# A sum formed one stage earlier, one load less in a second product on two queues, and pieces of an output product put between other products

## The chip, the cores and the metric

One core of a Trainium2 chip runs the kernel. The figure is the device time of one launch in microseconds; of the kernel before there are three runs, and their median is 7700.91 (7690.25 to 7706.97). TensorE multiplies, VectorE (DVE), ScalarE (ACT) and GpSimd (POOL) compute elementwise, and transfers between HBM and on-chip memory are issued into queues by SyncE (SP), ScalarE and GpSimd and carried by 16 DMA engines.

## The reference

`x` has shape (2, 96, 256, 256). Layer 0 adds to `x` a transformer block on its group-normalised copy; layer 1 adds a clustering block. Cut to what matters:

```python
x = x + _L0_conv_ref(_gn(x), ...)    # layer 0
x = x + _L1_conv_ref(_gn(x), ...)    # layer 1, clustering

def _L0_conv_ref(x, ...):            # here x is _gn(x)
    # windows of 16x16, step 14, in 19 bands of 19 windows for each batch
    y = _layernorm(tok, norm1_w, norm1_b)
    attn = softmax(q @ k.T / 4)
    tok = (attn @ v) @ wproj + tok
    x2 = overlap_add(tok) * factors
    y = _gelu(_layernorm(x2) @ fc1_w + fc1_b)
    dw = _gelu(depthwise_5x5(y) + dw_b)
    y = y + dw
    return y @ fc2_w + fc2_b + x2

def _cluster_fwd(x, ...):            # f, v: 1x1 convolutions; 8 regions
    sim = sigmoid(beta + alpha * cos(centres, points))
    sim = sim * (one-hot of its maximum over the 4 centres)
    agg = (sim @ value + value_centres) / (sum(sim) + 1)
    return proj(agg.T @ sim)
```

So the input of layer 1, called x1 in the kernel, is the original input plus `x2` plus the second product of the MLP.

## The kernel before

The stages run one behind another, each in a block of its own with a barrier at its end: group-norm statistics, a small setup, layer norm (`layer_norm`, writes `y_attention`), `attention` (writes `x2`), `fc1` (writes `y_mlp`), `conv` (the depthwise convolution, writes `s_mlp`), `fc2` (the second product, writes `x1`), a setup of the clustering, and `cluster` (writes `out`). Within a block every engine runs a program written out by hand; semaphores order them. The order of the work is the order of the code: there is no scheduler.

`attention` goes through 38 bands (19 per batch) of 19 windows. `acc` holds, in two slots, the 16 rows of a band, 4096 numbers in each of 96 partitions. SP loads the rows of x into it (`load_x`), GpSimd scales them to the group-normalised input in pieces of two rows (`scale`, L534), adds each window's projected result (`add`, L557), and hands the last rows to the next band (L561). In each window GpSimd also multiplies the attention result by its reciprocals (`normalise`, L540 and L544), for which it waits for VectorE; in eight windows of a band it turns an eighth of the next band's columns (`turn_columns`, L527). SP stores the finished 14 rows as x2 when the band's last `add` is done, and also spreads queries and keys of the next band over the heads (`spread_heads`).

`fc2` works on 14 tiles of 5 or 4 blocks (`tile_rows`); a tile is two half tiles `v` (`jj` 0 or 1). A block gives, for each batch and each of two row pairs, two rows of 256 pixels. The partitions hold four groups `g` of 32 output channels; `g // 2` is the batch, and `grp` counts the three parts of the 96 channels. SP alone issues the loads: `load_x(k)` 12 transfers of x2 into `xa` and 12 of x into `xb`, each into 32 partitions, and `load_s(v)` the activations s in transfers into 128 partitions (`sa`) and 64 (`sbb`), with the pixels of a row kept in four phases `q` (pixel 4k+q). GpSimd adds `xb` to `xa` (L1297). TensorE multiplies chunks of two rows (512 columns), four products with `sa` and four with `sbb` for each `grp` (L1317, L1320); the moving operand is read in the order

```python
.rearrange("c q (t k b) -> c b t k q", t=count, b=B)[:, b, :, 0:COLS, :]
```

so that neighbouring columns lie a whole line of a phase apart (650 numbers, 2600 bytes), and the pixels come out in natural order. VectorE adds bias, product and `xa` (L1336) and sums for the next group norm (L1342); ScalarE squares (L1354) and then issues the 12 stores of a tile (L1361).

`cluster` goes through 4 halves `f` of 4 segments of 8 steps `u`. In a step TensorE forms the products of a unit (L1720, two halves of four products), which ScalarE reads out (L1805 to L1808) and VectorE norms (L1846). A segment later, at the steps of `TURN_AT` (two turns at steps 3, 4 and 5, one at 6 and 7), `turn` transposes and aggregates (L1737, L1743), VectorE copying the result into `smt` (L1875). One half later, `piece` multiplies `smt` with the weights of the half (L1768) and VectorE adds the result into `xv` (L1904): two pieces in each of 48 steps (`pieces_at`: steps 3 to 7 of three segments and step 3 of one, for three halves), and the 32 pieces of the last half one behind another at the end (`rest`). Each piece uses the same two banks, so it waits until VectorE has added the piece before. The last lines of a step are

```python
                for a in pieces:
                    piece(*a)
```

in TensorE's program and the same with `added` in VectorE's.

## Time and profile before

| | |
|---|---|
| median of three runs | 7700.91 us (7690.25 to 7706.97) |
| the profiled execution's own time | 7690.68 us |
| its span, from first to last instruction | 7688.9 us |
| busy: TensorE, VectorE, ScalarE, GpSimd | 6602.4, 4890.2, 3553.5, 2457.7 us |
| mean granted clock of TensorE, as a share of 2.4 GHz | 0.932 |
| moved by DMA | 1252.80 MB |

The profile is of one execution. A busy time is the time in which an instruction of the engine runs; idle time before an instruction is put down to what ended it (`<-`). PE is TensorE's products, PEld its weight loads. One product of 32-bit numbers is two PE instructions. L1317 is line 1317 of the kernel. Names of buffers are shortened: `f_` is `fc2` (and `fc1`), `cl_` and `c_` the clustering, `at_` attention; x there stands for x2 and x1 as well.

### The profile page before, as it was taken

Reading aid. Unit: us, or ns where it says so; the run is one execution under the profiler, and the core shown is the slowest. Engines: PE = TensorE matmul, PEld = TensorE weight load, DVE = VectorE, ACT = ScalarE, POOL = GpSimd, SP = SyncE. Lnnn points to the kernel's source line nnn. Section 1 sums busy time; section 2 is a strip of 40 time slices with the busy share of each in tenths; the row PEclk is TensorE's granted clock in tenths of the full one; section 3 lists DMA queues with packets and bytes.
Section 4 is the critical chain, followed back from the end, with each engine's and each line's share of the span. In section 5 each row is a group of like instructions: output and inputs, shape, how many; then the busy total and the mean of one; then the engine's idle time right before and its main releaser. Section 6 shows DMA issues by size and latency. Waiting matters only on the chain. (4 is left out here: it accounts for less than half of the span.)

```text
span 7688.9 us, 138214 instructions
## 1 busy us (share of the span) xinstructions
PE 6602.4 (86%) x52604; PEld 3232.1 (42%) x52604; DVE 4890.2 (64%) x7370; ACT 3553.5 (46%) x5600; POOL 2457.7 (32%) x3173
## 2 busy tenths in 40 slices
PE   0886999999999999999997898899957768688885
PEld 0332555555555555555553333555500000476662
DVE  6785777777777777777774555788812222454554
ACT  0553666666666666666664666344401101243330
POOL 0443444444444444444445565000012222000000
PEclk9997999999999999999998999999988989787885
DMA  7784333334333434333325886988799999345655
GB/s 300 196 239 124 77 77 78 88 85 91 79 71 73 88 83 92 83 77 77 78 46 155 254 250 206 359 342 344 282 249 274 248 272 250 97 112 140 172 147 164
DMA packets 480460, 1252.80 MB, mean 163 GB/s; under 512 B 159620, under 2 KB 164740, under 8 KB 442628
## 3 DMA queue, kind: packets, MB, share of 16 engines
q1 hardware_dynamic: 444276, 1141.72, 54.3%
q0 software_dynamic: 7168, 50.34, 2.1%
q10 hardware_dynamic: 28368, 51.91, 1.8%
q8 instruction: 431, 7.06, 0.4%
q14 instruction: 217, 1.78, 0.1%
HBM read 731.14 MB, written 458.07 MB: 155 GB/s over the span
## 5 line engine op out<-in xcount | busy, mean ns | idle before, releaser
L727 DVE TENSOR_REDUCE at_mz<-at_ps 128x4 bf16<-128x1024 f32 x1444 | 1774.6, 1229 | 782.5 <-PE at_ps L651 782.2
L600 ACT ACTIVATE at_E<-at_ps 128x1024 f32<-128x1024 f32 x1444 | 1500.9, 1040 | 794.7 <-PE at_ps L663 794.7
L663 PE MATMUL at_ps<-at_qaug,at_k 32*128 32x256 f32 x11552 | 830.0, 401 | 79.2 <-DVE at_qaug L751 79.2
L674 PE MATMUL at_ps<-at_E,at_vaug 128*32 128x256 f32 x11552 | 774.3, 386 | 0.0
L1190 PE MATMUL cv_ps<-cv_yin,cv_band 128*128 128x384 f32 x2304 | 745.4, 486 | 27.9 <-DMA cv_yin<-y_mlp 27.9
L1210 DVE TENSOR_TENSOR cv_yin<-cv_gl,cv_yin 64x384 f32<-64x384 f32 x1152 | 637.5, 553 | 150.8 <-ACT cv_gl L1201 142.9
L663 PEld LDWEIGHTS at_ps<-at_qaug,at_k 32*128 32x128 f32 x11552 | 523.1, 184 | 443.1 <-issue 224.5
L1297 POOL TENSOR_TENSOR f_xa<-f_xa,f_xb 128x3840 f32<-128x3840 f32 (+1 forms) x28 | 213.2, 7636 | 1544.1 <-DMA f_xb<-in_x 1544.1
L540 POOL TENSOR_TENSOR at_share<-at_rden,t_share 128x8 f32<-128x8 f32 x722 | 146.8, 203 | 1558.8 <-DVE at_rden L738 1558.6
L1336 DVE SCALAR_TENSOR_TENSOR f_xa<-f_ps,f_b,f_xa 128x512 f32<-128x512 f32 (+1 forms) x216 | 136.2, 687 | 753.6 <-PE f_ps L1320 753.6
L1317 PE MATMUL f_ps<-f_sa,f_wa 128*32 128x512 f32 (+1 forms) x1728 | 379.8, 958 | 268.2 <-DMA f_sbb<-s_mlp 268.2
L651 PE MATMUL at_ps<-at_k,at_q 32*128 32x256 bf16 x5776 | 579.1, 277 | 8.9 <-DMA at_k<-at_packed 7.4
L1190 PEld LDWEIGHTS cv_ps<-cv_yin,cv_band 128*128 128x128 f32 x2304 | 436.1, 189 | 337.5 <-DMA cv_yin<-y_mlp 28.8
L1201 ACT ACTIVATE cv_gl<-cv_ps,cv_bias 128x384 f32<-128x384 f32 x576 | 334.4, 581 | 438.2 <-PE cv_ps L1190 438.2
L1720 PE MATMUL cl_ps<-c_rhs,cl_xu 97*128 97x208 f32 x2048 | 504.1, 416 | 21.9 <-ACT cl_dots L1808 19.6
L1354 ACT ACTIVATE f_squared<-f_xa 128x1280 f32<-128x1280 f32 (+1 forms) x84 | 99.1, 1180 | 895.1 <-DVE f_xa L1336 893.3
L681 PEld LDWEIGHTS at_ps<-t_wv,at_y 96*128 96x128 f32 x2888 | 377.1, 190 | 297.8 <-issue 297.8
L1720 PEld LDWEIGHTS cl_ps<-c_rhs,cl_xu 97*128 97x128 f32 x2048 | 463.6, 239 | 86.6 <-issue 76.2
L557 POOL TENSOR_TENSOR at_acc<-at_prs,at_acc 96x256 f32<-96x256 f32 x722 | 495.3, 686 | 3.1 <-ACT at_prs L606 3.1
L681 PE MATMUL at_ps<-t_wv,at_y 96*128 96x96 f32 x2888 | 495.5, 294 | 0.1
L686 PE MATMUL at_ps<-at_ot,t_wproj_heads 128*96 128x256 f32 x1444 | 485.4, 418 | 2.2 <-ACT at_prs L606 1.8
L544 POOL TENSOR_TENSOR at_on<-at_turned,at_share 128x256 f32<-128x256 f32 x722 | 444.3, 615 | 105.5 <-DVE at_ot L744 2.6
(210 smaller groups left out, 9570.2 us busy)
## 6 DMA issues: line engine op xcount, KB each, us to landing
cv_yin<-y_mlp SPq DMA_DIRECT2D x48, 2340.0 KB, 14.7
s_mlp<-cv_yin SPq DMA_DIRECT2D x48, 2340.0 KB, 8.4
at_rows_in<-y_attention SPq DMA_DIRECT2D x38, 1536.0 KB, 9.4
gn_xin<-in_x SPq DMA_DIRECT2D x16, 3072.0 KB, 23.2
ln_xin<-in_x SPq DMA_DIRECT2D x192, 256.0 KB, 7.6
y_attention<-ln_xin SPq DMA_DIRECT2D x192, 256.0 KB, 3.8
cl_xu<-x SPq DMA_DIRECT2D x128, 384.0 KB, 3.8
cl_xv<-x SPq DMA_DIRECT2D x64, 768.0 KB, 5.5
```

The source lines that it names most:

```text
L544: pool.tensor_tensor(on[:, s, :].rearrange("p (a d) -> p a d", d=VC), turned[:, s, :].rearrange("p (a d) -> p a d", d=VC), share[:, s, :]. ...
L557: pool.tensor_tensor(a, prs[:, m % 2, :].rearrange("p (r c) -> p r c", c=PS), a, ALU.add).then_inc(added, 1)
L600: act.activation(E[:, m % 2, 2 * p:2 * p + 2, :], psum[:, 2 + 2 * p:4 + 2 * p, :], ACT.Exp).then_inc(exp_done, 1)
L651: i = pe.matmul(psum[:, g, TOK * j:TOK * j + TOK], q_upper[rows, n % 2, tokens(w, 128 * j, 128)], k_upper[rows, n % 2, tokens(w)], start=T ...
L663: i = pe.matmul(psum[:, 2 + h, TOK * j:TOK * j + TOK], k[rows, n % 2, tokens(w, 128 * j, 128)], qaug[rows, m % 2, :], start=True, stop=True)
L674: i = pe.matmul(pv_ps[32 * h:32 * h + VC, 0:TOK], vaug[:, m % 2, z, h, :], E[:, m % 2, h, z * TOK:(z + 1) * TOK], start=(z == 0), stop=(z ...
L681: i = pe.matmul(lin_ps[:, j * C:(j + 1) * C], y[0:C, n % 2, tokens(w, 128 * j, 128)], t["wv"][:], start=True, stop=True)
L686: pe.matmul(lin_ps[0:C, 0:TOK], t["wproj_heads"][:], ot[:, m % 2, :], start=True, stop=True).then_inc(proj_done, 1)
L727: dve.tensor_reduce(mz[:, m % 2].rearrange("p j (h c) -> p h j c", c=32)[:, 2 * p:2 * p + 2, :, DQ], psum[:, 0:2, :].rearrange("p h (j n) ...
L1190: m = pe.matmul(psum[:, n % NB, 0:3 * RUN], band[:, s, c, a, :], yin[:, s, c, 3 * u:3 * u + 3, GAP * a:GAP * a + RUN], start=(a == 0), sto ...
L1210: i = dve.tensor_tensor(yc, gl[half_rows(f), n % NG, :].rearrange("p (t n) -> p t n", n=RUN), yc, ALU.add)
L1720: m = pe.matmul(psum[:, 2 * half + g // 2, 256 * (g % 2):256 * (g % 2) + NFC], xu[:, n % XS, 128 * tile:128 * tile + 128], t["rhs"][:, f * ...
```

## The change

It has five parts.

1. `attention` also forms xs = x + x2. SP loads the finished rows of x a second time, into a new buffer `xr`; GpSimd adds `acc` to it in pieces of two rows (`both`), one per window from window 5 of the next band on, and all eight pieces of the last band behind its last window; SP stores `xr` as xs. The scaling of a band's fresh rows, until now one piece per window in the band before from window 11 on, is done in the first four windows of the band itself, two pieces in each.
2. `fc2` loads xs only: `xb` and GpSimd's addition are gone, and `xa` has three slots for two.
3. In `fc2` SP and ScalarE each issue half of the loads and half of the stores (batch 0, partitions 0 to 63, from SP; batch 1 from ScalarE; of s the one row pair each).
4. TensorE in `fc2` reads phase by phase ("phases outside"), in steps of two numbers, so that a row comes out in phase order; VectorE's addition then takes one row per instruction and puts each pixel in its place, in steps of four numbers.
5. In `cluster` the first piece of a step goes between the two halves of the products and the second between the two turns, in VectorE's program alike.

In the layer norm and in the clustering several semaphores are also merged into others that already counted the step before or after (`log_done` into `rs_done`; seven of the weights' chain into `lhs_steps` and `lhs_taken`); the waits stay in the same places.

```diff
@@ -488,17 +497,22 @@
             for i in range(YP // 2):
                 spread_heads(0, i)
             for n in range(NB + 1):
+                if n >= 1:
+                    rows = own_rows(n - 1)
+                    if n >= 2:
+                        sp.wait_ge(xs_stored, 16 * (n - 1))
+                    sp.dma_start(xr[:, 0:rows * W], rows_of(x, n - 1, 0, rows)).then_inc(xr_loaded, 16)
                 if n + 1 < NB:
                     spread_heads(n + 1, 0)
                 if n >= 1:
-                    r = (n - 1) % NWIN
                     sp.wait_ge(added, NWIN * n)
-                    rows = STEP if r < NWIN - 2 else 2 if r == NWIN - 2 else PS
                     sp.dma_start(rows_of(x2, n - 1, 0, rows), acc[:, (n - 1) % 2, 0:rows * W]).then_inc(stored, 16)
                 if n + 1 < NB:
                     spread_heads(n + 1, 1)
                     spread_heads(n + 1, 2)
                 if n >= 1:
+                    sp.wait_ge(summed, sums(n - 1))
+                    sp.dma_start(rows_of(xs, n - 1, 0, rows), xr[:, 0:rows * W]).then_inc(xs_stored, 16)
                     sp.wait_ge(stored, 16 * n)
                     if n + 1 < NB:
                         if carries(n):
...
@@ -560,6 +575,13 @@
                     pool.wait_ge(added, m + 1)
                     pool.tensor_copy(acc[:, (n + 1) % 2, 0:(PS - first) * W], acc[:, n % 2, first * W:]).then_inc(carried, 1)
+            def both(n, piece):
+                if piece == 0:
+                    pool.wait_ge(added, NWIN * (n + 1))
+                    pool.wait_ge(xr_loaded, 16 * (n + 1))
+                rows = slice(piece * 2 * W, (piece + 1) * 2 * W)
+                pool.tensor_tensor(xr[:, rows], xr[:, rows], acc[:, n % 2, rows], ALU.add).then_inc(summed, 1)
             for piece in range(YP):
                 turn_columns(0, piece)
             for piece in fresh(0):
@@ -570,11 +592,15 @@
                 if n >= 5:
                     add(n - 5)
                 nb, w = where(n)
-                if nb + 1 < NB:
-                    if 2 <= w < 2 + YP:
-                        turn_columns(nb + 1, w - 2)
-                    if w >= 11 and w - 11 < len(fresh(nb + 1)):
-                        scale(nb + 1, fresh(nb + 1)[w - 11])
+                if nb + 1 < NB and 2 <= w < 2 + YP:
+                    turn_columns(nb + 1, w - 2)
+                if 1 <= nb < NB:
+                    for piece in fresh(nb)[2 * w:2 * w + 2]:
+                        scale(nb, piece)
+                    if 5 <= w < 5 + own_rows(nb - 1) // 2:
+                        both(nb - 1, w - 5)
+            for piece in range(own_rows(NB - 1) // 2):
+                both(NB - 1, piece)
         @block.scalar
...
@@ -1228,19 +1255,51 @@
+        def load_x(queue, k, half):
+            count = tile_rows(k)[2]
+            if k >= XA:
+                queue.wait_ge(stored[k % XA], 16 * XLOADS * (k // XA))
+            for grp in range(CGRP):
+                for rr in range(2):
+                    g = 2 * half + rr
+                    queue.dma_start(xa[32 * g:32 * g + 32, k % XA, grp, 0:count].rearrange("c t j w -> c t (j w)"),
+                                    group_rows(xs, k, half, rr, grp)).then_inc(xa_loaded[k % XA], 16)
+        def load_s(queue, v, half):
+            for row, t, at, count in row_sources(v // 2, half, v % 2):
+                n = count * PITCH - GAP
+                run = slice(at * PITCH, at * PITCH + n)
+                for f in range(2):
+                    src = sdr[:, f, row, :, t:t + count, :].rearrange("c e t n -> c e (t n)")[:, :, GAP * f:GAP * f + n]
+                    queue.dma_start(sa[:, v % 2, half, 2 * f:2 * f + 2, run], src[0:128]).then_inc(s_loaded[v % 2], 16)
+                    queue.dma_start(sbb[64 * half:64 * half + 64, v % 2, 2 * f:2 * f + 2, run], src[128:MLP]).then_inc(s_loaded[v % 2], 16)
+        def store(queue, k, half):
+            count = tile_rows(k)[2]
+            queue.wait_ge(x1_done, first[2 * k + 2])
+            queue.wait_ge(squares_done, CGRP * (2 * k + 2))
+            queue.wait_ge(sums_done, 2 * k + 2)
+            for grp in range(CGRP):
+                for rr in range(2):
+                    g = 2 * half + rr
+                    queue.dma_start(group_rows(x1, k, half, rr, grp),
+                                    xa[32 * g:32 * g + 32, k % XA, grp, 0:count].rearrange("c t j w -> c t (j w)")).then_inc(stored[k % XA], 16)
         @block.sync
         def _(sp):
...
@@ -1250,51 +1309,19 @@
...
+            load_x(sp, 0, 0)
+            load_s(sp, 0, 0)
+            load_s(sp, 1, 0)
             for k in range(NTILE):
                 if k + 1 < NTILE:
+                    load_x(sp, k + 1, 0)
+                    sp.wait_ge(f_done, first[2 * k + 1])
+                    load_s(sp, 2 * k + 2, 0)
+                    sp.wait_ge(f_done, first[2 * k + 2])
+                    load_s(sp, 2 * k + 3, 0)
+                store(sp, k, 0)
+            for u in range(XA):
+                sp.wait_ge(stored[u], 16 * XLOADS * len(range(u, NTILE, XA)))
...
@@ -1304,7 +1331,7 @@
                 def lines(a, b):
-                    return a[:, :, b0 * PITCH:b0 * PITCH + count * PITCH].rearrange("c q (t k b) -> c b t k q", t=count, b=B)[:, b, :, 0:COLS, :]
+                    return a[:, :, b0 * PITCH:b0 * PITCH + count * PITCH].rearrange("c q (t k b) -> c b t q k", t=count, b=B)[:, b, :, :, 0:COLS]
...
@@ -1327,41 +1354,50 @@
-                if n == first[v]:
-                    dve.wait_ge(xs_done, v + 1)
+                if n == first[v] and jj == 0:
+                    dve.wait_ge(xa_loaded[k % XA], 16 * XLOADS * (k // XA + 1))
                 dve.wait_ge(f_done, n + 1)
                 for grp in range(CGRP):
-                    xc = xa[:, k % 2, grp, b0:b0 + count, jj, :]
-                    pc = psum[:, CGRP * (n % 2) + grp, 0:count * W].rearrange("p (t w) -> p t w", w=W)
-                    i = dve.scalar_tensor_tensor(out=xc, in0=pc, scalar=b2[:, grp:grp + 1], in1=xc, op0=ALU.add, op1=ALU.add)
+                    for row in range(count):
+                        xc = xa[:, k % XA, grp, b0 + row, jj, :].rearrange("p (k q) -> p q k", q=PHASES)
+                        pc = psum[:, CGRP * (n % 2) + grp, row * W:row * W + W].rearrange("p (q k) -> p q k", q=PHASES)
+                        i = dve.scalar_tensor_tensor(out=xc, in0=pc, scalar=b2[:, grp:grp + 1], in1=xc, op0=ALU.add, op1=ALU.add)
                 i.then_inc(x1_done, 1)
                 if n + 1 == first[v + 1]:
                     dve.wait_ge(x1_done, n + 1)
...
+            load_x(act, 0, 1)
+            load_s(act, 0, 1)
+            load_s(act, 1, 1)
+            for k in range(NTILE):
+                if k + 1 < NTILE:
+                    load_x(act, k + 1, 1)
+                    act.wait_ge(f_done, first[2 * k + 1])
+                    load_s(act, 2 * k + 2, 1)
+                squares(2 * k)
+                if k + 1 < NTILE:
+                    act.wait_ge(f_done, first[2 * k + 2])
+                    load_s(act, 2 * k + 3, 1)
+                squares(2 * k + 1)
+                store(act, k, 1)
+            for u in range(XA):
+                act.wait_ge(stored[u], 16 * XLOADS * len(range(u, NTILE, XA)))
...
@@ -1772,8 +1806,16 @@
             for seg, u, turns, pieces in steps():
                 f, s = seg // SU, seg % SU
                 if seg < SEGS:
-                    products(seg * UPS + u)
-                for a in turns:
+                    products(seg * UPS + u, 0)
+                for a in pieces[0:1]:
+                    piece(*a)
+                if seg < SEGS:
+                    products(seg * UPS + u, 1)
+                for a in turns[0:1]:
+                    turn(*a)
+                for a in pieces[1:2]:
+                    piece(*a)
+                for a in turns[1:2]:
                     turn(*a)
                 if f and s == 0 and u == UPS - 1:
                     combined(f - 1)
...
@@ -1910,10 +1948,18 @@
                 if seg and u == 0:
                     similar(seg - 1)
                 if seg < SEGS:
-                    norms(seg * UPS + u)
+                    norms(seg * UPS + u, 0)
+                for a in pieces[0:1]:
+                    added(*a)
+                if seg < SEGS:
+                    norms(seg * UPS + u, 1)
                 if seg and u == 0:
                     choose(seg - 1)
-                for a in turns:
+                for a in turns[0:1]:
+                    turned(*a)
+                for a in pieces[1:2]:
+                    added(*a)
+                for a in turns[1:2]:
                     turned(*a)
                 if f and s == 0 and u == UPS - 1:
                     normalised(f - 1)
```

Three places show how the rows of an engine's program stand before and after; a row names the line, the operation, the buffers and the shape, and `x6` counts equal rows.

SP's program in `fc2` before, from the last transfers of one half tile's s to the next: `f_xa` and `f_xb` are the buffers of x2 (shown as `x`) and x (`in_x`), `f_sa` and `f_sbb` those of s.

```order
L1277 DMA f_sa<-s_mlp 128x2x648
L1278 DMA f_sbb<-s_mlp 64x2x648
L1259 DMA f_xa<-x 32x4x512 x12
L1265 DMA f_xb<-in_x 32x4x512 x12
L1277 DMA f_sa<-s_mlp 128x2x518
L1278 DMA f_sbb<-s_mlp 64x2x518
```

And ScalarE's after, at the same tile (SP's has the same transfers for batch 0, without the squares of L1382): L1301 stores a tile, L1279 loads xs.

```order
L1301 DMA x<-f_xa 32x4x512 x6
L1279 DMA f_xa<-xs 32x4x512 x6
L1289 DMA f_sa<-s_mlp 128x2x518
L1290 DMA f_sbb<-s_mlp 64x2x518
L1289 DMA f_sa<-s_mlp 128x2x518
L1290 DMA f_sbb<-s_mlp 64x2x518
L1382 ACTIVATE f_squared,squares<-f_xa 128x1280 x3
L1289 DMA f_sa<-s_mlp 128x2x518
L1290 DMA f_sbb<-s_mlp 64x2x518
L1289 DMA f_sa<-s_mlp 128x2x518
L1290 DMA f_sbb<-s_mlp 64x2x518
L1382 ACTIVATE f_squared,squares<-f_xa 128x1280 x3
```

The loads of s are shared out over two programs, the 12 transfers of `xb` are gone, and the stores now stand in both programs ahead of the loads of the tile after the next one.

TensorE's program in a step of `cluster` with two turns, before: L1720 is `products`, L1737 and L1743 a turn, L1768 two pieces.

```order
L1720 MATMUL cl_ps<-c_rhs,cl_xu 128x208 x8
L1737 MATMUL cl_ps<-c_eye,cl_sm 16x128 x8
L1743 MATMUL cl_ps<-cl_val,cl_sm 16x97 x8
L1737 MATMUL cl_ps<-c_eye,cl_sm 16x128 x8
L1743 MATMUL cl_ps<-cl_val,cl_sm 16x97 x8
L1768 MATMUL cl_ps<-cl_smt,cl_lhs 96x512 x4
```

And after, where the same lines are L1754, L1771, L1777 and L1802:

```order
L1754 MATMUL cl_ps<-c_rhs,cl_xu 128x208 x4
L1802 MATMUL cl_ps<-cl_smt,cl_lhs 96x512 x2
L1754 MATMUL cl_ps<-c_rhs,cl_xu 128x208 x4
L1771 MATMUL cl_ps<-c_eye,cl_sm 16x128 x8
L1777 MATMUL cl_ps<-cl_val,cl_sm 16x97 x8
L1802 MATMUL cl_ps<-cl_smt,cl_lhs 96x512 x2
L1771 MATMUL cl_ps<-c_eye,cl_sm 16x128 x8
L1777 MATMUL cl_ps<-cl_val,cl_sm 16x97 x8
```

The two pieces no longer stand next to each other, and the two turns have a piece between them.

GpSimd's program in `attention`, windows 11 and 12 of a band before (L540 and L544 `normalise`, L557 `add`, L534 `scale`):

```order
L540 TENSOR_TENSOR at_share<-at_rden,t_share 128x8
L544 TENSOR_TENSOR at_on<-at_turned,at_share 128x256
L557 TENSOR_TENSOR at_acc<-at_prs,at_acc 96x16x16
L534 TENSOR_SCALAR at_acc<-at_acc,t_gn_scale,t_out_shift 96x512
L540 TENSOR_TENSOR at_share<-at_rden,t_share 128x8
```

And after, windows 2 and, after the dots, 5 of the band itself (L555 and L559 `normalise`, L572 `add`, L542 `turn_columns`, L549 `scale`, L583 `both`):

```order
L555 TENSOR_TENSOR at_share<-at_rden,t_share 128x8
L559 TENSOR_TENSOR at_on<-at_turned,at_share 128x256
L572 TENSOR_TENSOR at_acc<-at_prs,at_acc 96x16x16
L542 COPY at_y<-at_rows_in 96x512
L549 TENSOR_SCALAR at_acc<-at_acc,t_gn_scale,t_out_shift 96x512 x2
...
L555 TENSOR_TENSOR at_share<-at_rden,t_share 128x8
L559 TENSOR_TENSOR at_on<-at_turned,at_share 128x256
L572 TENSOR_TENSOR at_acc<-at_prs,at_acc 96x16x16
L542 COPY at_y<-at_rows_in 96x512
L583 TENSOR_TENSOR at_xr<-at_xr,at_acc 96x512
```

Two scalings and a column turn now share a window, and a sum takes the place of the scaling beside the later column turns.

## Rows read from the trace of the kernel before

**Rows 1.** The view of windows by stage: us, busy time (and count) by engine, clock, DMA share, GB/s.

```profile
637.00:4080.00 3443.00, 3319.80 (x35264) 1709.62 (x35264) 2588.91 (x4335) 2126.93 (x3192) 1592.25 (x2765) 0.99 0.36 79
5590.00:6588.00 998.00, 728.73 (x3456) 68.13 (x3456) 246.19 (x300) 106.85 (x168) 213.23 (x28) 0.87 0.98 253
6571.00:6588.00 17.00, 0.00 (x0) 0.00 (x0) 3.36 (x3) 3.33 (x6) 0.00 (x0) 0.50 0.62 185
6640.00:7555.00 915.00, 746.71 (x6513) 593.03 (x6512) 474.69 (x768) 313.95 (x831) 23.95 (x47) 0.82 0.51 138
7555.00:7689.00 134.00, 70.16 (x174) 14.97 (x174) 49.70 (x77) 0.00 (x0) 8.59 (x17) 0.52 0.60 182
```

**Rows 2.** The same view, of stretches with one kind of transfer.

```profile
20.00:120.00 100.00, 0.00 (x0) 0.00 (x0) 94.56 (x158) 0.00 (x0) 0.00 (x0) 1.00 1.00 430
4900.00:5500.00 600.00, 600.00 (x1860) 351.31 (x1859) 514.57 (x930) 269.83 (x465) 0.00 (x0) 1.00 0.89 344
5600.00:5630.00 30.00, 0.00 (x0) 0.00 (x0) 0.00 (x0) 0.00 (x0) 6.58 (x1) 0.50 1.08 231
6180.00:6190.00 10.00, 0.00 (x0) 0.00 (x0) 0.00 (x0) 0.00 (x0) 10.00 (x2) 0.50 1.05 400
```

**Rows 3.** DMA of the second product, by queue: packets, MB, share of 16 engines.

```profile
q1 hardware_dynamic: 104259, 201.77, 83.7%
q10 hardware_dynamic: 27264, 50.34, 13.7%
```

**Rows 4.** Groups by line, second product (L1018: `fc1`): busy us, mean ns | idle, releaser.

```profile
L1317 PE MATMUL f_ps<-f_sa,f_wa 128*32 128x512 f32 x1344 | 328.5, 1057 | 268.2 <-DMA f_sbb<-s_mlp 268.2
...
L1018 PE MATMUL f_ps<-f_x,f_w 32*128 32x512 f32 x1344 | 168.3, 632 | 20.9 <-ACT f_ya L1057 20.8
...
L1336 DVE SCALAR_TENSOR_TENSOR f_xa<-f_ps,f_b,f_xa 128x256 f32<-128x256 f32 x48 | 20.3, 479 | 62.5 <-PE f_ps L1320 62.5
```

**Rows 5.** Groups by line, VectorE: a contiguous row, an addition of a piece, steps of 16 bytes.

```profile
L751 DVE TENSOR_TENSOR at_qaug<-at_ps,at_q 128x256 f32<-128x256 f32 x722 | 306.6, 425 | 57.8 <-PE at_ps L693 3.9
...
L1904 DVE SCALAR_TENSOR_TENSOR cl_xv<-cl_ps,c_proj_b,cl_xv 96x512 f32<-96x512 f32 x256 | 179.8, 742 | 183.4 <-PE cl_ps L1768 183.4
...
L1863 DVE TENSOR_TENSOR cl_hit<-cl_hit 128x256 f32<-128x256 f32 x16 | 10.0, 625 | 0.5
```

**Rows 6.** Groups by line, GpSimd, in attention and (L298) in the layer norm.

```profile
L527 POOL COPY at_y<-at_rows_in 96x512 f32<-96x512 f32 x304 | 325.9, 1073 | 4.9 <-DMA at_rows_in<-y_attention 4.9
...
L544 POOL TENSOR_TENSOR at_on<-at_turned,at_share 128x256 f32<-128x256 f32 x722 | 444.3, 615 | 105.5 <-DVE at_ot L744 2.6 <-POOL at_share L540 0.4
...
L534 POOL TENSOR_SCALAR at_acc<-at_acc,t_gn_scale,t_out_shift 96x512 f32<-96x512 f32 x256 | 195.8, 765 | 172.3 <-DMA at_acc<-in_x 172.3
...
L298 POOL TENSOR_TENSOR ln_sq<-ln_xin 128x1536 f32<-128x1536 f32 x64 | 175.7, 2746 | 289.1 <-DVE ln_xin L354 289.1
```

**Rows 7.** Timeline of GpSimd in attention: start us, us, instruction [idle before <- releaser].

```profile
1753.10 0.20 POOL L540 TENSOR_TENSOR at_share<-at_rden,t_share 128x8 f32<-128x8 f32 x1 [2.01 <-DVE at_rden L738]
...
1754.02 0.73 POOL L557 TENSOR_TENSOR at_acc<-at_prs,at_acc 96x256 f32<-96x256 f32 x1
...
1757.43 0.20 POOL L540 TENSOR_TENSOR at_share<-at_rden,t_share 128x8 f32<-128x8 f32 x1 [1.93 <-DVE at_rden L738]
```

**Rows 8.** DMA issues: count, KB each, median us to landing.

```profile
at_acc<-in_x SPq DMA_DIRECT2D x34, 1344.0 KB, 8.9
```

**Rows 9.** Timeline of TensorE in the clustering, four steps of two or one turns.

```profile
7068.99 3.08 PE L1720 MATMUL cl_ps<-c_rhs,cl_xu 97*128 97x208 f32 x16
...
7241.96 4.76 PE L1720 MATMUL cl_ps<-c_rhs,cl_xu 97*128 97x208 f32 x16
...
7248.31 0.63 PE L1737 MATMUL cl_ps<-c_eye,cl_sm 128*16 128x128 f32 x16 [0.70 <-DVE cl_smt L1875]
...
7251.82 1.10 PE L1768 MATMUL cl_ps<-cl_smt,cl_lhs 16*96 16x512 f32 x4 [1.51 <-DVE cl_xv L1904]
...
7285.42 0.80 PE L1720 MATMUL cl_ps<-c_rhs,cl_xu 97*128 97x208 f32 x3
```

162 lines of the change are left out of this document (57 added, 105 removed).

## The prediction, made before the changed kernel ran

> **What bounds the kernel now.** I read the stages first, from the view of windows [rows 1]. Attention takes 3443 us with TensorE busy for 3320 of them at a granted clock of 0.99, and its DMA engines are busy only 0.36 of the time. The second product (`fc2`, from the end of the convolution to 6588 us) takes 998 us with the DMA engines at a share of 0.98 and only 253 GB/s; TensorE is busy for 729 of them. The clustering loop takes 915 us, TensorE busy 747 and the clock 0.82; after it stand 134 us of pieces alone. The change touches these three stages. The rest (statistics, layer norm, `fc1`, convolution) keeps its instructions. There, and in the clustering, semaphores are merged into one another with the same order of increments, which I cost at nothing: the producers already follow one another.
>
> Next, why 0.98 of the DMA time moves only 253 GB/s. In [rows 2] the same 16 engines moved 430 GB/s at the start, where each load fills 128 partitions, and 344 over 600 us of the convolution, loads and stores of 128 partitions mixed. In the first 30 us of `fc2`, where nothing but loads of x2 and x into 32 partitions at a time is in flight, they are full (1.08) and give 231. And at 6180, where ACT's queue stores x1 (32 partitions too) while SP's queue loads, the same full engines give 400. So full engines do not mean a full rate, and a second queue beside SP's has gone with a high one. The queue view [rows 3] says the same over the stage: SP's queue carries 201.8 MB in 0.837 of 1000 us (241 GB/s), ACT's 50.3 MB in 0.137 (367 GB/s).
>
> **fc2, DMA.** Of the 252.1 MB it drops the load of x, 50.3 (as much as the x1 stores that ACT's queue carries), and leaves 201.8 MB [rows 3]. With nothing else changed the loads would need 837 us less 50.3 MB at 231 GB/s (218 us), so 619, and the stores 137: 756 us. At 400 GB/s throughout it would be 505 us. The two queues now each load half the batch into other partitions (0 to 63 from SP, 64 to 127 from ACT), which no stretch here shows with loads alone on both. I take 335 GB/s, just under the convolution's 344, since most loads of s fill 128 partitions as there, and the x loads, which do not, are a quarter of the bytes. That gives 602 us. About 20 us stand around it, where little can be in flight: the last half tile through TensorE, VectorE, ScalarE and its store, now 17 us at a DMA share of 0.62 behind the last product (6571 to 6588 in [rows 1]). Together 622 us, 376 less than 998.
>
> **fc2, does an engine become the bound?** The 14 tiles hold 64 blocks (eight tiles of five, six of four), so a tile of five is 15.8 MB, 47 us at 335 GB/s.
> TensorE: four products of 512 columns are eight instructions, 1344 instructions cost 328.5 us, so 1.96 us for eight [rows 4]. A tile of five blocks has 24 such groups and 12 of 256 columns, 30 in all by halves, 59 us: over 47. But the new order of the moving operand runs through k first, in steps of 8 bytes, where the old one jumped 2600 bytes at every element. `fc1`'s product of the same 512 columns, read without gaps, costs 168.3 us for 1344 instructions [rows 4]. By that row the stage's TensorE work falls from 729 to 373 us and a tile to 30. A step of 8 bytes stands between the two rows; I take the nearer, the contiguous one, and keep 729 as the other end.
> The Trainium skill (SBUF — State Buffer, Door 1) says that two accesses within one 16-byte line keep the full rate; by it the 8-byte step costs nothing and the stage is at 373, and without it at 729. No row here has that step.
> VectorE: 216 additions become 384 of one row each, read and written in steps of 16 bytes. A contiguous one of 256 elements takes 479 ns now [rows 4]; the nearest row with steps of 16 bytes has 625 ns where a contiguous one has 425 [rows 5], so I take 680 ns. All 384 are then 261 us (184 at 479 ns); even with the whole of today's 246 us [rows 1] left beside them VectorE has 507 us of work in 622. ScalarE is busy for 107 of 998 us [rows 1] and takes over half of the loads' issues, 20 per tile; an issue that lasts waits for room behind transfers, and hides under them. The third buffer of x lets a store come one tile late. So none of them is the bound, and since a tile's products need 30 of its 47 us, the buffers of s are free again well before the queues run dry.
>
> **Attention.** GpSimd adds 256 sums `both` of 96x512, and the 256 scalings move to the first four windows of a band. From 615 ns for 256 elements and 2746 for 1536 [rows 6] one `both` is about 1.05 us. GpSimd waits about 2 us in a window of 4.33 for the reciprocals [rows 7]. The fullest window after (column turn and two scalings) holds 0.20+0.62+0.65+1.07+2x0.77 = 4.1 us; the sums fall into windows without scalings, 3.6 us of work. `normalise` is needed one window later, so 0.1 us of lateness costs nothing. DMA: 100.7 MB more in 3443 us, from 79 to 108 GB/s on engines at 0.36, hidden. SP waits for the sums of a band before the next x load, but that is at window 11, and the load (8.9 us [rows 8]) is wanted seven windows of 4.33 us later. If that cover were gone, each band would pay the load, 37 x 9 us. What shows is the end: eight sums of the last band before the last store, +8.4 us, say 9.
>
> **Clustering.** 48 steps carry two pieces each. [rows 9] begins with one, at 7241.96: products 4.76 us (the 16 instructions take 3.08 at full clock, at 7068.99), two turns of some 1.1 us (the first half of one 0.63) with a wait of 0.70 for `smt` between them, a piece of 1.10, a wait of 1.51 for VectorE's two additions (0.74 each [rows 5]), a piece. In the new order products or a turn stand between the pieces, and a piece between the two turns: 2.5 us of TensorE's work against 1.5 of VectorE's, so both waits are covered. Waits alone: 48 x 1.51 and 27 x 0.70, 91 us. Products of 4.76 run in part at 1.2 GHz, behind those waits; the stage has 0.82 [rows 1]. If the clock holds at 2.4 GHz once they are gone, a step of two turns takes 3.0+2.2+2.2 = 7.4 us and one of one turn 6.3: four steps 27.4 against the 43.5 from 7241.96 to 7285.42 [rows 9]. Nine segments are 145 us, the 12 other steps at 2.2 us of waits 26: 171. The rows do not tell which; I take the middle, 130. The last 134 us, pieces alone, keep their order and time.
>
> **Sum.** 7690.7 (profiled execution) + 9 - 376 - 130 = 7194. That execution is 10 us under the median shown, 7700.9, so I forecast 7204, rounded to 7205.
>
> **Rivals.**
> *A, the forecast* (0.58): 7090 to 7290.
> *B, the second queue does not help the loads* (0.25). For it: all engines are full already at 231 GB/s [rows 2], and the 400 was a load beside a store, not two loads. Against: half-filled partitions are all that the 231 and the 430 differ in. Then `fc2` is 756+20 = 776 us, and the total 7690.7+9-222-130+10, about 7358.
> The Trainium skill speaks for B: SBUF — State Buffer ("Can I just issue two DMAs to hit both halves?") measured only 6% more for two loads at partitions 0 and 64, and DMA: Bandwidth & Descriptors (Rules for kernel authors) says that spreading over queues saves issue time alone. By them B's 7358 holds.
> *C, the 8-byte step reads as slowly as the old one* (0.06). For it: no row with that step. Then TensorE is busy 729 us at 59 us per tile, over the DMA's 47; with 25 us ahead and 20 behind, 774: about 7356.
> *D, the clustering gains nothing* (0.08): pieces and products share VectorE's queue, and an addition that waits for its piece now holds back the norms of the second half. Then the total is 7690.7+9-376+10, about 7334.
> *E, slower than before* (0.02). `both` waits in GpSimd's queue at window 5 for the load of x; behind it stand `normalise` and `add`, and behind them TensorE. It covers one window, 4.3 us, and would have to lose the whole gain, 497 us, over 37 bands, so the load must land 17.7 us late in each. It is issued some ten windows ahead (over 40 us) and takes about 9 us, like the present one; against it, then, a reserve of over 30 us.
> The change not doing what it says has 0.01: the load of x is gone from the queue's order.
>
> **How the numbers follow.** The time is A's. Best corner: 505+20 in `fc2` (-473) and -171, with 9 and 10 added 7066; worst of B with the waits alone, about 7400. Range 7090 to 7400: it leaves out the best corner, and C or B together with D. A alone reaches from 7090 to 7290. A measurement of this kernel tells about 0.2% (15 us) from no change. Faster 0.97 (A to D), same 0.01, slower 0.02 (E).
>
> **What the profile after would show.** `fc2` with one load of x per tile, in about 620 us at a DMA share near 1 and above 320 GB/s; under 280 GB/s B is right. The product of 512 columns under 700 ns instead of 1057 [rows 4]; if over 1000, C. VectorE's one-row addition at 480 to 680 ns. In attention the window still 4.33 us, with no wait of GpSimd for `xr`, and 9 us more at the end. In the clustering no 1.51 us waits ahead of the pieces but in the tail, and steps of 7.4 and 6.3 us if the granted clock rises from 0.82 to near 1. The forecast is wrong if the loads on two queues stay below 280 GB/s, or if issues held by a full queue keep ScalarE from its squares so long that stores, and with them the x buffers, come late.

## The result and the profile after

The changed kernel takes 7233.65 us (median of four runs, 7221.24 to 7236.30); the kernel before, with one run more than stated above, 7695.58 (four runs, 7675.86 to 7706.97). The ratio is 0.9392 with a 95% interval of 0.9372 to 0.9411. The forecast was 7205, with 7090 to 7290 for its own case. The profiled execution took 7235.98 us, its span 7234.2: 454.7 less than the span before.

The view of windows by stage, of the changed kernel: us, busy time (and count) of TensorE, its weight loads, VectorE, ScalarE and GpSimd, granted clock, DMA share, GB/s. The rows are attention, the first 33 us of `fc2`, `fc2`, the clustering loop and its tail.

```profile
634.00:4108.00 3474.00, 3332.49 (x35264) 1714.43 (x35264) 2588.90 (x4335) 2127.70 (x3192) 1907.13 (x3021) 0.98 0.47 107
5607.00:5640.00 33.00, 0.00 (x0) 0.00 (x0) 0.00 (x0) 0.00 (x0) 0.00 (x0) 0.50 1.01 248
5616.00:6294.00 678.00, 438.02 (x3456) 69.27 (x3456) 336.52 (x468) 106.83 (x168) 0.00 (x0) 0.82 1.01 297
6346.00:7100.00 754.00, 656.69 (x6515) 517.97 (x6513) 472.66 (x768) 315.57 (x831) 23.96 (x47) 0.91 0.59 168
7100.00:7234.00 134.00, 70.31 (x182) 14.98 (x174) 50.01 (x77) 0.00 (x0) 8.59 (x17) 0.52 0.60 182
```

Beside [rows 1] the reader sees three changes. `fc2` goes from 998 us to 678 (5616 to 6294), its DMA engines as full as before (1.01 for 0.98) but at 297 GB/s for 253. The clustering loop goes from 915 us to 754, TensorE's clock from 0.82 to 0.91; the tail stays at 134. And attention is longer, 3474 for 3447 (from its first to its last instruction, 3474.7 for 3446.8).

From the first to the last instruction of each stage:

| stage | before | after | difference | forecast |
|---|---|---|---|---|
| attention | 3446.8 | 3474.7 | +28 | +9 |
| `fc2` | 1006.6 | 686.8 | -320 | -376 |
| `cluster` | 1054.5 | 893.4 | -161 | -130 |
| all others together | 2180.1 | 2178.5 | -2 | 0 |

The queues of the second product, of the changed kernel (packets, MB, share of 16 engines), to set beside [rows 3]: each carries half, and together they take the whole of the engines' time.

```profile
q1 hardware_dynamic: 52432, 101.28, 50.9%
q10 hardware_dynamic: 51441, 99.81, 49.5%
```

The groups by line of the changed kernel: busy us, mean ns of one | idle before it, and what ended that. L1344 is the product of 512 columns, L1364 VectorE's one-row addition, L583 GpSimd's sum `both`.

```profile
L1344 PE MATMUL f_ps<-f_sa,f_wa 128*32 128x512 f32 x1344 | 204.1, 680 | 239.9 <-DMA f_sbb<-s_mlp 238.3 <-DVE f_xa L1364 1.5
...
L1364 DVE SCALAR_TENSOR_TENSOR f_xa<-f_ps,f_b,f_xa 128x256 f32<-128x256 f32 x384 | 227.0, 667 | 345.7 <-PE f_ps L1347 344.9
...
L583 POOL TENSOR_TENSOR at_xr<-at_xr,at_acc 96x512 f32<-96x512 f32 x256 | 323.9, 1266 | 0.1
```

The product fell from 1057 ns to 680 and the addition takes 667 (680 was forecast). TensorE waits 238 us for `sbb`, so the transfers still set the length of the stage. The sum `both` costs 1.27 us where 1.05 was taken.

A step of the clustering with two turns, from TensorE's timeline of the changed kernel (start us, us, instruction):

```profile
6800.94 1.67 PE L1754 MATMUL cl_ps<-c_rhs,cl_xu 97*128 97x208 f32 x8
6802.54 1.10 PE L1802 MATMUL cl_ps<-cl_smt,cl_lhs 16*96 16x512 f32 x4
6803.57 1.67 PE L1754 MATMUL cl_ps<-c_rhs,cl_xu 97*128 97x208 f32 x8
6805.18 0.63 PE L1771 MATMUL cl_ps<-c_eye,cl_sm 128*16 128x128 f32 x16
6805.62 0.52 PE L1777 MATMUL cl_ps<-cl_val,cl_sm 128*16 128x97 f32 x16
6806.07 1.10 PE L1802 MATMUL cl_ps<-cl_smt,cl_lhs 16*96 16x512 f32 x4
6807.10 0.63 PE L1771 MATMUL cl_ps<-c_eye,cl_sm 128*16 128x128 f32 x16
6807.55 0.52 PE L1777 MATMUL cl_ps<-cl_val,cl_sm 128*16 128x97 f32 x16
6807.99 1.67 PE L1754 MATMUL cl_ps<-c_rhs,cl_xu 97*128 97x208 f32 x8
```

No row has an idle time before it. The step lasts 7.06 us (6800.94 to 6808.00), where in [rows 9] four steps took 43.5; the steps of one turn last 6.16. The waits of the same stage, from the chain of waits (us in total, times, longest):

```profile
PE cl_ps L1754 <- DMA cl_xu<-x: 33.6, 10, 5.2
...
PE cl_ps L1771 <- DVE cl_smt L1913: 16.1, 19, 2.2
...
PE cl_ps L1802 <- DVE cl_xv L1942: 1.8, 2, 1.1
```

The wait of a piece for its additions has gone to 1.8 us. Another has grown: ten times the products wait for their load, 33.6 us in all, where it was 2.2 before.

### The profile page after: what moved, and what is told of

The parts are those of the page before. It is cut to its first block and busy times, and to the rows that moved or that the text cites. A ratio compares the mean times of both kernels' runs of the same rounds, so it can differ in the third digit from the quotient of the medians.

```text
span 7234.2 us, 138671 instructions
## 1 busy us (share of the span) xinstructions
PE 6229.6 (86%) x52604; PEld 3161.5 (44%) x52604; DVE 4977.8 (69%) x7538; ACT 3555.8 (49%) x5600; POOL 2561.1 (35%) x3401
## 3 DMA queue, kind: packets, MB, share of 16 engines
q8 instruction: 432, 7.08, 0.4%
q14 instruction: 219, 1.79, 0.1%
## 5 line engine op out<-in xcount | busy, mean ns | idle before, releaser
L555 POOL TENSOR_TENSOR at_share<-at_rden,t_share 128x8 f32<-128x8 f32 x722 | 146.9, 204 | 1444.7 <-DVE at_rden L764 1444.6
L572 POOL TENSOR_TENSOR at_acc<-at_prs,at_acc 96x256 f32<-96x256 f32 x722 | 495.1, 686 | 3.1 <-ACT at_prs L632 3.1
L559 POOL TENSOR_TENSOR at_on<-at_turned,at_share 128x256 f32<-128x256 f32 x722 | 444.1, 615 | 104.4 <-DVE at_ot L770 1.3
L1754 PE MATMUL cl_ps<-c_rhs,cl_xu 97*128 97x208 f32 x2048 | 445.4, 375 | 40.1 <-DMA cl_xu<-x 33.6
L1364 DVE SCALAR_TENSOR_TENSOR f_xa<-f_ps,f_b,f_xa 128x256 f32<-128x256 f32 x384 | 227.0, 667 | 345.7 <-PE f_ps L1347 344.9
L1754 PEld LDWEIGHTS cl_ps<-c_rhs,cl_xu 97*128 97x128 f32 x2048 | 395.1, 210 | 109.8 <-issue 67.3
L1344 PE MATMUL f_ps<-f_sa,f_wa 128*32 128x512 f32 (+1 forms) x1728 | 236.3, 619 | 239.9 <-DMA f_sbb<-s_mlp 238.3
L632 ACT ACTIVATE at_prs<-at_ps 96x256 f32<-96x256 f32 x722 | 426.9, 591 | 3.9 <-PE at_ps L712 3.6
```

Source lines behind the costliest of these rows:

```text
L559: pool.tensor_tensor(on[:, s, :].rearrange("p (a d) -> p a d", d=VC), turned[:, s, :].rearrange("p (a d) -> p a d", d=VC), share[:, s, :]. ...
L572: pool.tensor_tensor(a, prs[:, m % 2, :].rearrange("p (r c) -> p r c", c=PS), a, ALU.add).then_inc(added, 1)
L1754: m = pe.matmul(psum[:, 2 * half + g // 2, 256 * (g % 2):256 * (g % 2) + NFC], xu[:, n % XS, 128 * tile:128 * tile + 128], t["rhs"][:, f * ...
```

## The experiments

Each experiment is one edit of the changed kernel (the transfers by themselves are a program of their own). Its total is set against the changed kernel's 7233.65 us, but the kernel before, measured beside the experiments again, had medians of 7703 to 7707 us in place of 7696: differences of some 10 us between totals say little. Spans of stages are from one profiled execution each; where a stage's program is unchanged they show how far chance goes. `fc2` took 682 to 691 us in the four kernels in which it is the changed kernel's (692 and 701 in two where it reads x2), attention 3473 to 3484 in nine, the clustering 887 to 893 in ten.

### One queue for the loads

All loads of `fc2` on SP, all stores on ScalarE, as before; xs, the third buffer and the phases outside stay.

```diff
...
-                    load_x(sp, k + 1, 0)
-                    sp.wait_ge(f_done, first[2 * k + 1])
-                    load_s(sp, 2 * k + 2, 0)
-                    sp.wait_ge(f_done, first[2 * k + 2])
-                    load_s(sp, 2 * k + 3, 0)
-                store(sp, k, 0)
+                    for half in range(2):
+                        load_x(sp, k + 1, half)
+                    for v in (2 * k + 2, 2 * k + 3):
+                        sp.wait_ge(f_done, first[v - 1])
+                        for half in range(2):
+                            load_s(sp, v, half)
...
```

> The changed kernel, but all loads of the second product issued by SP and all its stores by ScalarE, as before the change; xs, three buffers of x and the phases outside stay. Theory P (the engines are full whichever queue feeds them, and the stage is as long as its packets take): the stage grows from 687 us by no more than what 248 against 231 GB/s does to the 50 MB of x, 15 us; 7235 to 7250 in all. Theory Q (loads into both halves of the partitions at once are what makes them faster): the stage goes to the 776 us of rival B, about 7322 in all.

Measured: 7291.74 us (7283.27 to 7306.23), and 750.0 us for `fc2`. The window of the stage in this kernel:

```profile
5616.00:6366.00 750.00, 441.03 (x3456) 69.27 (x3456) 336.02 (x469) 106.84 (x168) 0.05 (x1) 0.79 1.02 271
```

The engines are full (1.02) and give 271 GB/s for 297. So the second queue is worth 63 us: the 15 of theory P are too few, the 89 of Q too many. P rested on the 248 GB/s of the first 33 us, in which SP still loads weights; from 5620 to 5640, with both queues loading, the changed kernel moves 288. The other 257 of the 320 us come from the dropped load and what goes with it (the reading order, the third buffer); they are not split further here.

### Phases inside again

TensorE reads k innermost, VectorE adds two rows at once.

```diff
-...rearrange("c q (t k b) -> c b t q k", t=count, b=B)[:, b, :, :, 0:COLS]
+...rearrange("c q (t k b) -> c b t k q", t=count, b=B)[:, b, :, 0:COLS, :]
```

> The changed kernel, but TensorE reads k innermost in jumps of 2600 bytes again and VectorE adds in chunks of two rows, as before the change. If TensorE's 438 us become the 729 of before, a tile of five blocks needs 59 us of TensorE against 49 of DMA, and the stage grows from 687 to 775 or more: 7320 or more in all. If the transfers alone set the stage (theory P with TensorE hidden), it stays within 10 us of 7234.

Measured: 7354.77 us (7348.06 to 7360.23), `fc2` 807.4. The window and the product's group in this kernel:

```profile
5617.00:6424.00 807.00, 728.29 (x3456) 67.90 (x3456) 246.15 (x300) 106.86 (x168) 0.00 (x0) 0.95 0.80 252
```

```profile
L1344 PE MATMUL f_ps<-f_sa,f_wa 128*32 128x512 f32 x1344 | 328.3, 1056 | 71.4 <-DMA f_sbb<-s_mlp 71.4
```

TensorE is busy for 728 of 807 us and the DMA share falls to 0.80: the bound has changed sides. Once the transfers had shrunk, the new reading order, with VectorE's additions that go with it, was worth 121 us. With the transfers of before it would have been hidden, as far as the busy time tells (729 of 998); no run shows that.

### The clustering's order back

Both pieces at the end of a step, in both programs; the rest as changed.

```diff
-                for a in pieces[0:1]:
-                    piece(*a)
                 if seg < SEGS:
                     products(seg * UPS + u, 1)
-                for a in turns[0:1]:
-                    turn(*a)
-                for a in pieces[1:2]:
-                    piece(*a)
-                for a in turns[1:2]:
+                for a in turns:
                     turn(*a)
...
+                for a in pieces:
+                    piece(*a)
```

> The changed kernel, but both pieces of a step stand at its end again, behind the turns, in TensorE's and VectorE's programs. If the order is the whole cause of the 161 us that the clustering lost, its span is 1054 us again and the time about 7395. If a part came from elsewhere (merged semaphores, what the second product leaves behind), less.

Measured: 7412.02 us (7401.65 to 7433.63), the clustering 1057.9. The chain of waits of the stage in this kernel:

```profile
PE cl_ps L1802 <- DVE cl_xv L1938: 70.9, 47, 1.5
PE cl_ps L1771 <- DVE cl_smt L1909: 34.3, 45, 2.2
```

The 70.9 us are back, and the stage has its old length (1054.5). The order is the whole cause, within the few us by which a stage varies; the merged semaphores cost and gain nothing that shows. The total is 17 us over the 7395 expected, of which the clustering has 3.

### The second piece last

```diff
-                for a in pieces[1:2]:
-                    piece(*a)
                 for a in turns[1:2]:
                     turn(*a)
...
+                for a in pieces[1:2]:
+                    piece(*a)
```

> The changed kernel, but the second piece of a clustering step stands at the step's end, behind both turns; the first stays between the products. The wait of the second turn for the copy of the first is open again (0.70 us in 27 steps), the wait of a piece for the additions is still covered. By waits alone 19 us more, 7253. If such a wait also brings TensorE's clock down, as behind the waits of before, the steps of two turns grow beyond 7.8 us and the time beyond 7275.

Measured: 7256.71 us (7251.52 to 7274.23), 23 more than the changed kernel. Steps of two turns take 7.82 us for 7.06. TensorE's timeline of such a step:

```profile
6805.15 0.63 PE L1771 MATMUL cl_ps<-c_eye,cl_sm 128*16 128x128 f32 x16
6805.60 0.52 PE L1777 MATMUL cl_ps<-cl_val,cl_sm 128*16 128x97 f32 x16
6806.81 0.63 PE L1771 MATMUL cl_ps<-c_eye,cl_sm 128*16 128x128 f32 x16 [0.70 <-DVE cl_smt L1913]
```

The wait of 0.70 is open again, and everything round it is as short as in the changed kernel: a half of the products 1.67 us, a piece 1.10. So one such wait costs about its own length in its step, and the clock stays. The steps that carry pieces are 19 us longer together, as the waits alone gave; the others are 8 us shorter in this execution, and the whole clustering is 904.4 for 893.4. In the kernel before, steps with both kinds of wait went in part at half clock; whether the waits of 1.51 us alone would do that, no run tells.

### Attention without its sum, and with the sum but not its transfers

In the first kernel attention is that of before, and `fc2` reads x2, so x is missing from x1. (Its diff, long, takes out all that part 1 of the change put in.)

> The changed kernel with the attention of before: no xs is formed, and the second product loads x2 in its place, so that x is missing from x1. The transfers of the second product are as large as in the changed kernel. If attention's 28 us more are the price of the sum, 7206; if 18 of them are chance of the one execution and only the last band's sums cost, 7225.

Measured: 7213.80 us (7206.90 to 7230.09), between the two expected values; the span of attention decides, 3445.6. The three executions without the sum's transfers have 3446 to 3447, the ten with them 3473 to 3487: so the 28 us are the price of forming xs, not chance; in the nine kernels with the same attention it is 27 to 37.

The second keeps GpSimd's program and SP's wait for it, and takes away the 100 MB:

```diff
-                    sp.dma_start(xr[:, 0:rows * W], rows_of(x, n - 1, 0, rows)).then_inc(xr_loaded, 16)
...
-                    sp.dma_start(rows_of(xs, n - 1, 0, rows), xr[:, 0:rows * W]).then_inc(xs_stored, 16)
...
-                pool.tensor_tensor(xr[:, rows], xr[:, rows], acc[:, n % 2, rows], ALU.add).then_inc(summed, 1)
+                pool.tensor_tensor(xr[:, rows], acc[:, n % 2, rows], acc[:, n % 2, rows], ALU.add).then_inc(summed, 1)
```

> The changed kernel, but attention's 256 sums add the finished rows to themselves: x isn't loaded a second time and xs isn't stored (the second product reads x2, and x is missing from x1). GpSimd's work, its order, and SP's wait for the sums ahead of the next band's load of x stay. If the 18 us of attention's 28 that lie ahead of its last band come from the 100 MB more that fill the DMA engines in windows 14 to 18, they go, and only the last band's sums stay: attention 3456, 7215 in all. If they come from GpSimd's fuller windows or from the later load of x, attention stays at 3475 and the time at 7234.

Measured: 7212.40 us (7196.51 to 7220.82), attention 3446.1. The windows of attention in this kernel:

```profile
637.00:4083.00 3446.00, 3317.79 (x35264) 1708.26 (x35264) 2587.72 (x4335) 2128.55 (x3192) 1852.34 (x3021) 0.99 0.37 79
```

GpSimd is busy for 1852 us in place of before's 1593 (1907 in the changed kernel, since a sum of one input twice takes 1.00 us for 1.27) and attention isn't a microsecond longer. The whole price hangs on the transfers. The 3456 expected for attention, 10 us more, were missed: here the last band's eight sums, 8.01 us, run beside the last store of x2 and are hidden. The price has two parts. At the end, in the changed kernel's timeline of GpSimd and SP, the eight last sums stand ahead of one more store:

```profile
4091.07 0.30 SPq L509 DMA_DIRECT2D x<-at_acc  x1
4091.12 9.79 POOL L583 TENSOR_TENSOR at_xr<-at_xr,at_acc 96x512 f32<-96x512 f32 x8
4100.93 0.30 SPq L515 DMA_DIRECT2D xs<-at_xr  x1
```

The last store starts 9.8 us later than x2's does; the forecast had 8.4, say 9. It is the store behind the sums that makes them show. The other 18 us lie in windows 14 to 18 of a few bands. The windows around one (band 21), and TensorE's timeline there, of the changed kernel:

```profile
2630.00:2635.00 5.00, 4.81 (x58) 2.67 (x56) 4.17 (x10) 3.20 (x6) 1.80 (x5) 1.00 0.99 202
2635.00:2640.00 5.00, 3.74 (x26) 1.51 (x22) 1.78 (x3) 1.41 (x3) 1.11 (x2) 0.78 1.06 171
2640.00:2645.00 5.00, 5.00 (x40) 2.80 (x42) 3.11 (x5) 1.47 (x3) 1.50 (x3) 0.50 0.99 226
```

```profile
2635.34 0.70 PE L689 MATMUL at_ps<-at_qaug,at_k 32*128 32x256 f32 x5 [0.18 <-DVE at_qaug L777]
...
2637.12 1.44 PE L689 MATMUL at_ps<-at_qaug,at_k 32*128 32x256 f32 x11 [1.07 <-issue]
```

In the midst of 16 equal products, with no data to wait for, TensorE stands still for 1.07 us; then its clock falls to 0.50 of 2.4 GHz, and that window takes 8.55 us in place of 4.33. The DMA engines are full (0.99 to 1.06): behind the wait for the sums SP issues the store of xs, the load of x, keys and queries, the load of y, the tap blocks and the second load of x one after the other, in one stretch of some 30 us. With the wait but without the 100 MB there is no such gap; the 100 MB without the wait were not tried.

What TensorE stands still for can be read from the packets of the queue that carries its instructions (q8 in the view of DMA). In band 21 one packet starts at 2613.0 and the next only at 2633.5, where the median distance is 11.5 us. It has landed at 2635.6, and TensorE goes on at 2637.12. The view of DMA from 2633 to 2636 has it (packets, MB, share of 16 engines); the view from 2614 to 2633 has none of q8:

```profile
q8 instruction: 1, 0.02, 4.4%
```

All five such gaps of 0.7 us or more in the changed kernel's attention end 1.3 to 1.8 us after an instruction packet has landed that came 17.5 to 20.5 us behind the one before it; over all kernels with the 100 MB it is 63 of 63 gaps, 1.3 to 2.0 us after a landing, where a moment of attention taken at random lies 1 to 2 us after one in some 9% of cases. So TensorE had run out of instructions, and the next ones came late.

### The tap blocks out of that stretch

```diff
                 if n >= 1:
+                    unroll_taps((n - 1) * PER_BAND, PER_BAND)
                     sp.wait_ge(added, NWIN * n)
...
-                if n >= 1:
-                    unroll_taps((n - 1) * PER_BAND, PER_BAND)
```

> The changed kernel, but SP issues the four transfers of the convolution's tap blocks of a band ahead of its wait for the band's last addition (about window 5), and no longer behind the loads of x and y (windows 14 to 18), where TensorE stood still for lack of instructions in six bands. If the long stretch of full DMA engines there is what holds its instructions back, these stalls go and attention falls from 3475 by 10 to 20 us: 7215 to 7225. If they come from the number of transfers in a band, they move to other windows and the time stays at 7234.

Measured: 7243.89 us (7240.97 to 7250.35), attention 3486.6. The expectation fell, and so did its rival, by which the stalls would have moved to other windows: more windows were late (16 by over 1 us, 6 in the changed kernel), again all among windows 14 to 18. Attention is 12 us longer than in the changed kernel, but only 3 above the longest of the same attention in the other kernels. Which transfer of the stretch matters isn't settled. What the traces add: in several of these kernels the gap stands at the same place of TensorE's program (band 5 window 15, 16 window 15, 21 window 14, 22 window 14, 31 window 15), in others partly elsewhere, and in no execution without the 100 MB is there one of 0.7 us or more.

### The transfers by themselves

Sixteen kinds of transfer behind one another, some 5 MB each, with a barrier between; nothing is computed. This program was executed once.

```diff
+        phase("a_one_queue_32", p32((0, 2, 1, 3), S), [])
+        phase("b_two_queues_halves", p32((0, 1), S), p32((2, 3), S))
+        phase("c_two_queues_mixed", p32((0, 2), S), p32((1, 3), S))
...
+        phase("g_one_queue_32_spread", [spread(s, j) for s in S for j in range(4)], [])
```

> The transfers of the second product by themselves, one kind behind another with a barrier between, from x and a filled tensor shaped as s; nothing is computed, and the output holds copies of parts of x. Some 5 MB of each: 32 partitions a transfer on one queue; on two queues, each its half of the partitions; on two queues, halves mixed; 128 and 64 partitions a transfer with the same pieces of 2048 bytes; 32 partitions spread over all 128; 32 partitions in pieces of 10 KB; s into 128 partitions on one and two queues; s into 64 on one and two; stores on one and two; a load beside a store. If the partitions that a transfer covers set its rate: 231 GB/s for 32 adjoining ones, 400 or more for 128, and for 32 spread ones also near 400. If what it reads in HBM sets it (pieces of 2048 bytes a channel apart): 231 in all of these, and only the pieces of 10 KB are fast. If a second queue with the other half is what helps: 231 on one queue, over 350 on two with halves, 231 on two mixed.

Windows from the middle of each phase, where the engines are full (us, no engine busy, clock, DMA share, GB/s). In order: 32 adjoining partitions on one queue; on two, each its half; on two, halves mixed; 128 partitions; 64 on one queue; 64 on two, each its half; 32 spread over all 128; 32 in pieces of 10 KB; s into 128 on one queue, on two; s into 64 on one, on two; s into 128 and 64 in turn on one queue, and the part of that in which the two alternate; stores on one queue, on two; loads into 32 on one queue beside stores from 32 on the other.

```profile
44.00:62.00 18.00, 0.00 (x0) 0.00 (x0) 1.00 1.07 235
69.00:81.00 12.00, 0.00 (x0) 0.00 (x0) 1.00 1.06 333
88.00:106.00 18.00, 0.00 (x0) 0.00 (x0) 1.00 1.07 226
114.00:124.00 10.00, 0.00 (x0) 0.00 (x0) 1.00 1.05 402
130.00:150.00 20.00, 0.00 (x0) 0.00 (x0) 1.00 1.07 217
157.00:169.00 12.00, 0.00 (x0) 0.00 (x0) 1.00 1.05 333
177.00:188.00 11.00, 0.00 (x0) 0.00 (x0) 1.00 1.00 367
195.00:213.00 18.00, 0.00 (x0) 0.00 (x0) 1.00 1.02 221
221.00:230.00 9.00, 0.00 (x0) 0.00 (x0) 1.00 1.04 400
237.00:246.00 9.00, 0.00 (x0) 0.00 (x0) 1.00 1.04 399
253.00:272.00 19.00, 0.00 (x0) 0.00 (x0) 1.00 1.06 228
279.00:292.00 13.00, 0.00 (x0) 0.00 (x0) 1.00 1.04 311
299.00:318.00 19.00, 0.00 (x0) 0.00 (x0) 1.00 1.02 226
299.00:313.00 14.00, 0.00 (x0) 0.00 (x0) 1.00 1.03 238
325.00:341.00 16.00, 0.00 (x0) 0.00 (x0) 1.00 0.94 259
348.00:359.00 11.00, 0.00 (x0) 0.00 (x0) 1.00 1.03 352
366.00:376.00 10.00, 0.00 (x0) 0.00 (x0) 1.00 1.05 375
```

The source in HBM is out: pieces of 10 KB are no faster (221) than those of 2048 bytes (235), and the same pieces go at 367 when the 32 partitions are spread and at 402 when 128 are filled. Nor is it the number of partitions: 64 adjoining ones are no faster than 32 (217, 235). What counts is how they are spread, and over how much of the 128 what is in flight reaches at a time. A second queue helped the loads into 32 or 64 partitions when each queue kept to its half (333, 333 and 311; 226 with halves mixed, tried for 32 alone) and did nothing for those into 128 (400, 399). The stores gain in the same way (259, 352), and loads of 32 beside stores of 32, each on a queue of its own, reach 375. And wide transfers in turn with those into 64 partitions lose their advantage: 238 for the mix, where 400 and 228 for the shares of each would give 320 (an estimate from these rows). The longer window, 226, also holds the last four transfers into 64 partitions, which run by themselves.

### Halves mixed in the kernel

```diff
-                for rr in range(2):
-                    g = 2 * half + rr
+                for b in range(2):
+                    g = 2 * b + half
...
-                                    group_rows(xs, k, half, rr, grp)).then_inc(xa_loaded[k % XA], 16)
+                                    group_rows(xs, k, b, half, grp)).then_inc(xa_loaded[k % XA], 16)
```

> The changed kernel, but of xs SP loads the first row pair of both batches (partitions 0 to 31 and 64 to 95) and ScalarE the second, so that neither queue keeps to a half of the partitions; the loads of s and the stores stay. If the 63 us that the second queue is worth come from each queue keeping to its half, the second product goes from 687 us towards the 750 of one queue: 7260 to 7300. If it is the mixing of transfers of different kinds, no change: within 15 us of 7234.

Measured: 7284.17 us (7277.68 to 7285.40), `fc2` 730.9: 44 of the 63 us of the second queue go when the loads of x no longer keep to halves. That agrees with 333 and 226 above.

### Wide loads first

```diff
-            for row, t, at, count in row_sources(v // 2, half, v % 2):
...
+            for wide in (True, False):
+                for row, t, at, count in row_sources(v // 2, half, v % 2):
...
+                        if wide:
+                            queue.dma_start(sa[:, v % 2, half, 2 * f:2 * f + 2, run], src[0:128]).then_inc(s_loaded[v % 2], 16)
+                        else:
+                            queue.dma_start(sbb[64 * half:64 * half + 64, v % 2, 2 * f:2 * f + 2, run], src[128:MLP]).then_inc(s_loaded[v % 2], 16)
```

> The changed kernel, but each queue issues the loads of a half tile's s into 128 partitions first and then those into 64, in place of one after the other in turn. By the transfers measured alone, 67 MB into 128 partitions at 376 GB/s are 179 us and 34 MB into 64 on two queues at 295 are 114: 293 us for s in place of the 379 that its packets take now. If what is in flight at once sets the rate, and the two queues keep roughly in step, the second product falls by 40 to 86 us: 7148 to 7194. If only the mean over all partitions counts, nothing changes: within 15 us of 7234.

Measured: 7216.70 us (7201.67 to 7221.64), `fc2` 668.9: 18 us less, and 13 less than the shortest of the unchanged `fc2`, but under half of the lower bound. The order within a queue does little, presumably since the other queue is elsewhere; that wasn't shown.

### s in every second partition

The 64 channels go to partitions 0, 2, 4, ... (SP) and 1, 3, 5, ... (ScalarE); the weights of the other row pair are zero.

```diff
-                    queue.dma_start(sbb[64 * half:64 * half + 64, v % 2, 2 * f:2 * f + 2, run], src[128:MLP]).then_inc(s_loaded[v % 2], 16)
+                    queue.dma_start(sbb[half:128:2, v % 2, 2 * f:2 * f + 2, run], src[128:MLP]).then_inc(s_loaded[v % 2], 16)
...
-                        m = pe.matmul(psum[32 * g:32 * g + 32, bank, 0:w], wb[rows, outs], lines(sbb[rows, v % 2], g // 2), start=False, stop=True)
+                        m = pe.matmul(psum[32 * g:32 * g + 32, bank, 0:w], wb[:, g % 2, outs], lines(sbb[:, v % 2], g // 2), start=False, stop=True)
```

> The changed kernel, but the 64 channels of s that fill half the partitions lie in every second partition (even from SP, odd from ScalarE) in place of a lower and an upper half; TensorE multiplies them over all 128 partitions by weights that are zero for the other row pair. If the partitions that a transfer covers set its rate, as for the 32 spread ones (333 GB/s for 229), all of s moves at some 375 GB/s, 269 us in place of 379, and the second product falls by 70 to 110 us, if TensorE's products are not longer: 7124 to 7164. If the number of partitions counts and not where they lie, no change: 7234.

Measured: 7140.35 us (7134.32 to 7151.13); the ratio to the kernel before is 0.9263 (0.9240 to 0.9286). `fc2` takes 590.7 us. Its window and the two products in this kernel:

```profile
5609.00:6199.00 590.00, 383.96 (x3456) 123.02 (x3456) 336.24 (x468) 106.87 (x168) 0.11 (x1) 0.83 1.01 344
```

```profile
L1350 PE MATMUL f_ps<-f_sa,f_wa 128*32 128x512 f32 x1344 | 202.8, 671 | 197.5 <-DMA f_sbb<-s_mlp 188.6 <-DVE f_xa L1369 8.9
...
L1352 PE MATMUL f_ps<-f_sbb,f_wb 128*32 128x512 f32 x1344 | 198.0, 655 | 0.0
```

The same bytes with the same full engines (1.01) go at 344 GB/s for 297, and the product over 128 partitions costs 655 ns, no more than the other. The time lies within the 7124 to 7164 expected, so it is where the partitions lie that counts, and this version beats both kernels.

### Two buffers of x

```diff
-    XA = 3
+    XA = 2
```

> The changed kernel with two buffers of x in the second product, as before the change. SP's and ScalarE's queues then wait, ahead of a tile's loads of x, for the landing of the stores that stand right before them (12 to 19 us from issue to landing), with nothing else behind them in flight. If that empties the queues, 12 tiles lose some 13 us each: about 7390. If the loads of s that are still in flight cover it, less than 20 us: 7234 to 7254.

Measured: 7256.19 us (7243.59 to 7270.07), `fc2` 714.1 at a DMA share of 0.95: just above the range of the second case, and 23 us more than the longest of the unchanged `fc2`. The third buffer is worth some 25 us. The loads of s in flight cover most of the wait for the stores.

## Why the prediction was right, point by point

**What bounds the kernel.** Right: full engines at a low rate. The changed kernel shows 297 GB/s at 1.01, and the transfers alone show that the partitions are the reason why the stretch of 32 gave 231 and that of 128 gave 430 [rows 2]. That "half-filled partitions are all that the 231 and the 430 differ in" was not so when it was written: the pieces differed in length as well, and only the run with pieces of 10 KB (221) ruled that out. The row of 231 also isn't pure: from some 5622 us on loads of s are in it, and 5600 to 5620 alone has 221.

**fc2, DMA.** The mechanism was right, the rate was mis-sized. The step that erred is "I take 335 GB/s, just under the convolution's 344, since most loads of s fill 128 partitions as there": two thirds of the bytes of s do, but on their queue they stand in turn with transfers into 64 partitions, and the mix alone gives 238, near the 228 of the narrow ones. The stage ran at 297 for 335, 678 us for 622. With s in every second partition it runs at 344, and 590 us. That the alternation is what costs in the kernel isn't shown: with the wide loads first only 18 us went. Rival B, "the second queue does not help the loads", is refuted in its mechanism (63 us, 333 against 235 GB/s alone), and the time is 29 us from A's 7205 and 124 from B's 7358; the rate of 297 stands between the two signs given, 280 for B and 320 for A. The Trainium skill's 6% for two loads into the two halves (SBUF — State Buffer, "Can I just issue two DMAs to hit both halves?") isn't what these transfers show: 235 to 333 is 42%. Where page and runs differ, the runs decide.

**fc2, engines.** The 8-byte step reads nearly as fast as the contiguous row (680 against 632 ns, at a clock of 0.82), so C is refuted and the rule cited beside it for that step holds here; TensorE was busy for 438 us where 373 was worked out, still hidden. VectorE's 384 additions took 227 us where 261 was forecast. ScalarE issued 204 loads, half of them, 14.6 per tile; the prediction had over half and 20, which is near what it issues with its stores (20.6). That the new order is needed at all once x is dropped, phases inside again showed (+121 us).

**Attention.** +28 for +9. The last band's part was right (9.8). The failed step is "100.7 MB more ..., from 79 to 108 GB/s on engines at 0.36, hidden". The mean share hid that behind SP's wait for the sums the transfers stand packed in one stretch, in which TensorE's instructions at times come late. GpSimd's work and its fuller windows cost nothing, as forecast (shown with sums of 1.00 us in place of 1.27). Rival E's way (the load of x late for `both`) didn't occur: L583 waited 0.1 us in all.

**Clustering.** -161 for -130, inside the 91 to 171 stated. Both waits closed as forecast (pieces 70.9 to 1.8 us, `smt` 35.9 to 16.1), and the clock came back: products average 375 ns for 416. Steps are 7.06 and 6.16 us where 7.4 and 6.3 were worked out. The middle value was too low, because the clock came back in every step that carries pieces. The steps that carry pieces are 182 us shorter together, more than the upper bound of 171; 26 us were given back in the others, where the products now wait 33.6 us for their loads of x1 (2.2 before).

**Sum.** +28 - 320 - 161 = -453 against 454.7 of the span. With the -2 of the other stages that is the whole. The clustering's surplus of 31 us covers part of the 75 by which `fc2` (56) and attention (19) fell short: that the time came within 29 us of the forecast is in part the luck of errors of opposite sign.

## What to carry to other kernels

That the DMA engines are full says nothing of the rate: look at which partitions the transfers in flight write, and spread every transfer, or every pair on two queues, over all 128. Where there are only 64 channels, put them in every second partition and give the product zero weights for the others. When a wait is put ahead of loads, count what it packs together behind it, since a mean share of 0.5 says nothing of a stretch at 1, and TensorE's instructions come by DMA as well. Independent pieces of work put into an engine's waits return the waits and, if the waits had brought the clock down, the clock too.

## What the runs showed of the hardware beyond expectation

TensorE, with its data there, stood still for 1.07 us in the midst of equal products while the DMA engines were at 1.06, and gaps of 0.7 us or more only in kernels with that stretch of full engines; the window after it ran at half clock. The Trainium skill (Runtime: NRT & Kernel Launch, Instruction fetch mechanics) says that instructions come in blocks of 16 KB over a DMA queue of their own, and that this is mostly hidden. The traces agree with the blocks: one instruction queue, q8, carried 7.08 MB in 432 packets, 16.4 KB each (the other, q14, 1.79 MB in 219). They also show when it isn't hidden: every one of the 63 gaps ends 1.3 to 2.0 us after such a packet has landed, 57 of them behind a distance of 17.5 us or more to the packet before, where the median is 11.5. That the full engines are what makes the packet late rests on the three executions without the 100 MB, which have no such gap; how they do it isn't shown.

Wide transfers (400 GB/s alone) that alternate with ones into 64 partitions (228 alone) ran at 238 together. 32 partitions spread over the 128 load at 367, 64 adjoining ones at 217.
